# Two routing stages around an attention layer: PE's fillers, the top-six search and four shared products change places

## The reference

```python
x = x + 0.5 * ffn(layernorm(x))
x = x + attention(layernorm(x))
x = x + 0.5 * ffn(layernorm(x))

# ffn, on T = 2048 tokens of width 512, E = 64 experts, K = 6, CAP = 96
scores = sigmoid(x @ gate_w)                       # (T, 64)
scores_b = scores + bias
group_scores = sum of the two largest in each of 8 groups of 8
mask all but the 4 best groups
topk_ids = top_k(masked scores_b, 6); topk_w = scores at these ids
topk_w = topk_w / sum(topk_w) * 2.5
# each expert takes the first 96 tokens, in token order, that chose it
h = silu(buf @ w_gate) * (buf @ w_up)              # per expert, inner width 192
y = sum over the chosen experts of topk_w * (h @ w_down)
shared = (silu(x @ ws_gate) * (x @ ws_up)) @ ws_down
return y + shared
```

## Time and profile before

| | |
|---|---|
| median of 3 runs | 1400.79 us |
| profiled execution | 1399.98 us |
| its span, first to last instruction | 1397.8 us |
| PE busy | 1212.3 us (87%) |
| DVE busy | 620.0 us (44%) |
| ScalarE busy | 516.5 us (37%) |
| POOL busy | 507.5 us (36%) |
| mean granted clock of PE | 0.921 |
| read and written | 307.26 MB, mean 220 GB/s |

### The profile page before, as it was taken

How to read it: one execution, slowest core, us unless ns; L and a number is a source line. 1 busy time by engine, 2 the same in 40 slices (tenths; PEclk the granted TensorE clock), 3 DMA queues, 4 the chain that set the end, 5 groups by cost and what they waited for, 6 DMA issues and landing times.

```text
span 1397.8 us, 25616 instructions
## 1 busy us (share of the span) xinstructions
PE 1212.3 (87%) x10066; PEld 773.1 (55%) x10066; DVE 620.0 (44%) x1124; ACT 516.5 (37%) x1297; POOL 507.5 (36%) x413
## 2 busy tenths in 40 slices
PE   5999998888984668999999999889998998889880
PEld 4632776666762455565565565364435766657650
DVE  5775121221223676767867766533880221212220
ACT  1411211111110258888878878742211111111100
POOL 0022444544453643324324224000213544544544
PEclk9998999999997688899999999779986999999995
DMA  8995699999986934344444443232843999999957
GB/s 313 360 392 180 196 337 341 343 334 335 339 233 128 349 97 107 84 114 105 123 107 106 125 103 76 76 129 82 346 140 104 342 337 346 339 330 338 331 91 132
DMA packets 146199, 307.26 MB, mean 220 GB/s; under 512 B 17568, under 2 KB 50720, under 8 KB 146080
## 3 DMA queue, kind: packets, MB, share of 16 engines
q1 hardware_dynamic: 112960, 238.32, 50.5%
q0 software_dynamic: 23808, 57.69, 18.3%
q10 hardware_dynamic: 9312, 9.62, 2.0%
HBM read 222.47 MB, written 61.87 MB: 203 GB/s over the span
## 4 chain that ended last, share of the span: by engine, by line
PE 46%; DMA 27%; DVE 11%; issue 6%; ACT 4%; POOL 3%; SPq 1%; DVEq 0%; POOLq 0%; ACTq 0%
DMA ya_d<-osb,tok 13%; DMA out<-osb,tok 8%; PE ps L382 7%; PE ps L447 5%; PE ps L490 4%; DMA buf<-xn_d,tok 4%; PE ps L398 4%; PE ps L478 4%; PE ps L458 4%; PE ps L504 3%; PE ps L279 2%; PE ps L433 2%; DVE osb L976 2%; PE ps L365 2%; PE ps L271 1%
## 5 line engine op out<-in xcount | busy, mean ns | idle before, releaser
L382 PE MATMUL ps<-bufT,gu 128*64 128x96 f32 x6144 | 301.6, 261 | 0.0
L382 PEld LDWEIGHTS ps<-bufT,gu 128*64 128x64 f32 x6144 | 291.2, 176 | 9.2 <-issue 2.2
L976 DVE TENSOR_SCALAR osb<-ps,gt 96x512 f32<-96x512 f32 x128 | 94.1, 746 | 267.0 <-PE ps L398 75.2
L1045 DVE TENSOR_REDUCE Mx<-ps 128x1 f32<-128x512 f32 x256 | 170.4, 684 | 82.1 <-PE ps L458 81.4
L664 ACT COPY bufT<-ps 128x384 f32<-128x384 f32 x128 | 60.9, 478 | 346.1 <-PE ps L365 345.7
L704 ACT ACTIVATE ps<-ps,Mx 128x512 f32<-128x512 f32 x256 | 175.5, 688 | 35.7 <-DVE Mx L1045 34.9
L398 PE MATMUL ps<-wd,h 64*96 64x512 f32 x768 | 180.4, 602 | 3.2 <-DVE osb L976 3.2
L717 ACT ACTIVATE PT<-ps 128x512 f32<-128x512 f32 x256 | 159.0, 623 | 58.9 <-PE ps L478 57.7
L1161 POOL DMA_INDIRECT buf<-xn_d,tok x128 | 127.7, 998 | 93.9 <-issue 60.9
L458 PE MATMUL ps<-St 96*128 96x512 f32 x256 | 121.7, 490 | 19.5 <-ACT ps L704 18.8
L969 DVE TENSOR_TENSOR h<-sg,ps 128x288 f32<-128x288 f32 x64 | 29.1, 454 | 224.5 <-PE ps L382 224.5
(11 more groups left out here) (144 smaller groups left out, 1548.4 us busy)
## 6 DMA issues: line engine op xcount, KB each, us to landing
gu<-in_L_ffn_w_gate SPq DMA_DIRECT2D x64, 768.0 KB, 12.8
gu<-in_L_ffn_w_up SPq DMA_DIRECT2D x64, 768.0 KB, 15.7
wd<-in_L_ffn_w_down SPq DMA_DIRECT2D x64, 768.0 KB, 18.2
St<-HL SPq DMA_DIRECT2D x192, 128.0 KB, 2.3
wqk<-wp_d SPq DMA_DIRECT2D x32, 512.0 KB, 5.3
xn_d<-XN SPq DMA_DIRECT2D x24, 256.0 KB, 2.8
X<-in_L_attn_X SPq DMA_DIRECT2D x4, 1024.0 KB, 10.9
ya_d<-X SPq DMA_DIRECT2D x4, 1024.0 KB, 14.0
```

Of the source, the lines that this page charges most:

```text
L382: t = e.matmul(bk[64 * k:64 * k + 64, CAP * j:CAP * j + CAP], gu[:, 2 * k + m, c, j:F:3], f.bufT[(2 * q + k) % 4][:, c, :], start=(c == 0) ...
L976: e.tensor_scalar(f.osb[x % 4][:, :], bank(4 + x % 2)[0:CAP, :], f.gt[:, x % 8:x % 8 + 1], None, ALU.mult).then_inc(f_ev, 1)
L1045: e.tensor_reduce(Mx[:, qt, hl:hl + 1], bank((4, 5, 7)[n % 3]), AX, ALU.max, negate=True).then_inc(a_max, 1)
```

## The change

**PE, stage one.** Six products of X with itself into a bank that nobody reads (`pe_warm`) are issued when the first quarter of X has landed, and two more behind the first and the second group of four tiles. The gate part of shared group 0 stands behind the third group of tiles. The tiles are taken group by group right behind their root on DVE, ScalarE and PE; before, DVE was one group ahead. Three of the four weight splits move among them on ScalarE, the fourth behind the sigmoid, and its DVE part behind the key pass; SP stores that fourth part behind two expert loads.

**The top six.** The masked scores lie in rows of 66 columns, of which the last two are set to 3.0e38. The eight largest of a row are then these two and the six wanted. One `match_replace` puts 2.0e38 in the place of all eight, and "equal to 2.0e38" is the mask. The search for indices, the copy of the sixth index and four passes on DVE and three on POOL go; one pass on DVE and one on POOL come. The keys are smaller by the factor T and multiplied by T at the end.

**Shared expert.** Both stages use one order now: the keys' transposes stand before the last third of group 2, and all of group 0's down products behind it; the third multiply stands behind round 2 in both; the sums for the weights behind round 3. The list's transpose stands in the middle of group 2's down products. The four of group 3 go to the expert pairs: two behind the first gate and up product, two behind the first down product.

**The end of the attention.** The root of tiles 12 to 14 and these three tiles are issued on DVE before the last result, tile 15 has a root of its own, and PE does all of the rest of group 0 behind the logits.

The diff, cut to its core:

```diff
+        def pe_warm(e, n):
+            for _ in range(n):
+                e.matmul(bank(7), X[:, 0, 0:128], X[:, 0, :], start=True, stop=True)
+
         def pe(e):
+            e.wait_ge(s_x[0], 16)
+            pe_warm(e, 6)
             for g in range(4):
-                for i in range(4 * g - 4, 4 * g + 4 if g == 3 else 4 * g):
...
+                for i in range(4 * g, 4 * g + 4):
+                    pe_tile(e, f1, i)
+                    if i:
+                        pe_logits(e, f1, i - 1)
+                if g < 2:
+                    pe_warm(e, 2)
+                if g == 2:
+                    pe_shared_up(e, f1, 0, (0,))
...
             pe_attention(e)
-            pe_shared_up(e, f2, 0, (1, 2))
...
         def pe_route(e, f):
...
+            pe_shared_up(e, f, 0, (1, 2))
+            pe_shared_up(e, f, 1)
+            pe_shared_up(e, f, 2, (0, 1))
+            pe_keys(e, f)
+            pe_shared_up(e, f, 2, (2,))
+            pe_shared_down(e, f, 0)
+            pe_shared_down(e, f, 1)
+            pe_shared_up(e, f, 3)
+            pe_shared_down(e, f, 2, (0, 1))
+            pe_first(e, f)
+            pe_shared_down(e, f, 2, (2, 3))
...
         def pe_turned(e, f, x):
-            else:
-                e.wait_ge(f_shc, 16 * f.n + NT)
+            if x < 8:
+                e.wait_ge(f_shc, 16 * f.n + (12, 12, 14, 16)[x // 2])
...
         # pe_experts
+                if st in (1, 2):
+                    e.wait_ge(f_bTs, 64 * f.n + 2 * st + 2)
+                    pe_shared_down(e, f, 3, (2 * st - 2, 2 * st - 1))
...
         # act_route
+            e.preload_act_table(ACT.Sigmoid)
             e.wait_ge(f_lg, f.n + 1)
...
             if not f.n:
-                act_shared_silu(e, f, 0)
+                act_cast(e, 3)
...
         # dve_route
+            e.tensor_tensor(PM[:, :, 0:E].rearrange("p i (g j) -> p i g j", j=8), s8.rearrange("p (i g) j -> p i g j", g=NG),
+                            neg.rearrange("p (i g) -> p i g", g=NG).unsqueeze(3).to_broadcast([128, NT, NG, 8]), ALU.add)
+            e.memset(PM[:, :, E:E + 2], BIG).then_inc(f_step, 1)
...
             for i in range(NT):
+                t = e.match_replace(PM[:, i, :], f.V8[:, i, :], PM[:, i, :], MARK)
...
+            e.scalar_tensor_tensor(out=P1, in0=PM[:, :, 0:E], scalar=MARK, in1=bE(cst[:, C_TK:C_TK + 16]),
+                                   op0=ALU.is_equal, op1=ALU.add).then_inc(f_step, 1)
...
-                if r == 5:
+                if r == 3:
...
-                if r == 2 and not f.n:
+                if r == 2:
                     dve_shared_mul(e, f, 2)
...
         # dve_attention
+                    if u == NU and j == 12:
+                        dve_root(e, f2, 1)
+                        for i in range(12, 15):
+                            dve_tile(e, f2, i)
...
         # sp
+            for c in range(3):
+                store_part(e, c)
...
+            e.wait_ge(s_wd, 16 * 6)
+            for q in (1, 2):
                 load(e, f1, q)
+            store_part(e, 3)
             e.wait_ge(s_y, 64)
             load(e, f1, 4)
+            e.wait_ge(s_wd, 16 * 8)
+            load(e, f1, 3)
```

More of the change, by code:

```diff
@@ L755, in act @@
                 act_root(e, f1, g)
-                for i in range(4 * g - 4, 4 * g + 4 if g == 3 else 4 * g):
-                    if i >= 0:
-                        act_tile(e, f1, i)
-                        if i in (9, 11, 13, 15):
-                            c = i // 2 - 4
-                            e.wait_ge(s_wf[c], 16)
-                            e.copy(wh[c][:, :], wf[c][:, :].bitcast(F32)).then_inc(w_hi, 1)
+                for i in range(4 * g, 4 * g + 4):
+                    act_tile(e, f1, i)
+                    if i in (5, 8, 10):
+                        act_cast(e, (5, 8, 10).index(i))
             act_route(e, f1)
@@ L768, in act @@
             act_root(e, f2, 1)
-            act_shared_silu(e, f2, 0)
-            for i in range(12, NT):
+            for i in range(12, 15):
                 act_tile(e, f2, i)
+            act_root(e, f2, 2)
+            act_tile(e, f2, 15)
             act_route(e, f2)
@@ L841, in part @@
                 return flat(ap)[:, o:o + m * j].rearrange("p (m j) -> p m j", j=j)
-            if f.n:
-                dve_shared_mul(e, f, 0)
-            else:
+            if not f.n:
                 e.wait_ge(s_c, 32)
@@ L930, in dve_route @@
+            if not f.n:
+                dve_rest(e, 3)
             e.wait_ge(f_kT, f.n + 1)
@@ L1143, in dve @@
             dve_attention(e)
-            dve_root(e, f2, 1)
-            for i in range(12, NT):
-                dve_tile(e, f2, i)
+            dve_root(e, f2, 2)
+            dve_tile(e, f2, 15)
             dve_route(e, f2)
@@ L1375, in sp @@
             load(e, f1, 0)
-            store_parts(e)
+            for c in range(3):
+                store_part(e, c)
             for g in range(4):
```

181 lines of the change are left out of this document (68 added, 113 removed).

## The result

In paired runs the changed kernel took 1384.93 us (median of 13, 1374.52 to 1399.56) beside 1405.18 us for the kernel before (1393.35 to 1413.62): ratio 0.9875, 95% interval 0.9844 to 0.9907. The ratio is formed from the fast executions alone, so it is not the quotient of the two medians (0.9856). Forecast was 1386, range 1373 to 1398. The first profile of it, however, is of an execution of 1398.34 us (span 1396.5), only 1.3 us of span under the profile before (1397.8). So two profiles have to be compared stretch by stretch; each pair of end times would tell another story.

What follows compares the result with a forecast made beforehand. The expert stages' scatter-adds, with DMA saturated, were taken as the bound, so their start, set by the routing before, counts. The terms 11.0 + 4.9 - 2 = 14 us off 1399.98 gave 1386 us, range 1373 to 1398.

Steps and rivals of the forecast that it cites:

- L: End of the last router logits: forecast 46 us in stage one, against 53.7 before.
- the DVE stall: Key search, behind round 2: VectorE waits 4.3 us for the first four shared products before the third shared multiply.
- F: The list's transpose after the key search: forecast 110.8 us in stage one, a gain of 14.2.
- P0: End of the experts' first down product: forecast 141.3 us in stage one, a gain of 16.3.
- P1: End of the experts' second down product: forecast 154.2 us in stage one, a gain of 11.4.
- A: Start of the attention layer's first product; 11 us was taken as stage one's gain that reaches the end.
- R to K: Stage two, start of the attention layer's last result products to end of the key transposes: forecast 49.0 us.
- rival 1: The gap before the list's transpose does not lower TensorE's clock: 6 us a stage, 1374 us; chance 0.12.
- rival 2: Stage one's router tiles do not hold 2.4 GHz: 1412 us if all slow, chance 0.08; about 1397 if half, 0.12.
- The second scatter-add: Expert stage: it waits for the last shared result, some 6 us behind P0, which costs nothing.
- rival 3: Expert weights become the wait, or DMA engines run dry: 6 to 8 us given back, 1393 us; chance 0.15.
- The sum of 14: Whole kernel: 11.0 from stage one plus 4.9 from stage two minus 2 for clock falls, off 1399.98 us.

Runs made afterwards that it cites:

- e5: Changed kernel with the last four shared products put back ahead of the experts in both stages; ratio 0.9931 to the kernel before.
- e3: Changed kernel with three filler products in TensorE's idle time before the list's transpose, both stages; ratio 0.9892 to the kernel before.
- e4: Changed kernel with the third shared multiply moved from behind round 2 to behind round 4, both stages; ratio 0.9932 to the kernel before.
- e7: Changed kernel with the third multiply behind round 4 and the sixth expert pair's load held until two gathered blocks are transposed; ratio 0.9818 to the kernel before.
- e1: The changed kernel run again without edits, for a second profile; ratio 0.9913 to the kernel before.
- e2: Changed kernel without the ten warm products of stage one; ratio 0.9979 to the kernel before.
- e12: The kernel before the change, run again without edits for a second profile; that execution took 1412.3 us.
- e10: Changed kernel with third multiply behind round 4, sixth pair's load held, router weights earlier, and attention rows ahead of shared weights; ratio 0.9882 to the kernel before.
- e11: Changed kernel with only the sixth expert pair's load held until the first two gathered blocks are transposed; ratio 0.9918 to the kernel before.
- e6: Changed kernel with 5.5 us of VectorE passes that nobody reads added ahead of the key pass, both stages; ratio 0.9983 to the kernel before.

## Why the prediction was right

**Stage one, right in mechanism.** In the first profile: tiles at full clock from the first logits on, L 46 for 44.3, match_replace 3.2 for 3.15, the DVE stall, PE idle 3.6 for 3.37, F 110.8 for 108.6, P0 141.3 for 139.6, P1 154.2 for 152.7. The stall behind round 2 was 2.67, not 4.3: the last weight part's pass (2.60 beside GpSimd, not 1.76) stood between the key pass and the rounds, and delayed the rounds before they could wait. F-K hardly notices (38.3 for 38.9), because the stall ends where PE's first four products end. In stage two, which has no such pass, it was 4.02. In the second profile L was 49.0 and P1 157.7, and the gain at A 7.9 instead of 12.3; the 11 that I took lies between.

**Stage two, too much.** R to K is 52.4 us in both profiles, not 49.0. Two terms: L comes 1.0 later than I had it, and the matmuls behind the last gap run slow, which costs the 2.4 us that L to K takes more than in stage one (28.3 for 25.9). I had this as a subtraction of 2. P1-R gained 1.0 to 2.4, where 4.9 - 2 = 2.9 stood.

**The move of four products, right in sign.** e5 prices it by the profiles, 5 us a stage; the times leave it open. I had priced the pairs, not the move.

**No fall at F (rival 1), wrong in price.** I gave 6 us a stage if the gap passed. e3, e4 and e7 took the gap away, and against e1 P0-F came out 2.0 less (e3), 1.3 more (e4) and 1.1 less (e7) in stage one and within 0.2 in stage two, since the gather is next. I had written that the gather was hidden by the copy of a shared result; that held only as long as the products were slow.

**Slower tiles (rival 2), present.** Not the whole stretch, but from a wait of about 2 us to the next fillers, in five of nine profiles, 3 to 5 us each. The Trainium skill (TensorE: Matmul & The Clock Gate, Part 4: PE-mode transpose) has transposes not counting as busy in the same way. Here tiles that are one third transposes, with fillers between the groups, kept 2.4 GHz for 28 us once they had it (first profile). Without help they needed 28 us to get it in e2 and 31 in the first profile of before, which agrees with the page, but 7 us in e12, which does not. So the traces do not settle the rule: tiles can bring the clock up by themselves, and what makes it 7 us or 28 is open.

**The second scatter-add** waits for the last shared result, as I had it (four profiles name its store, `yb_d<-XN`, as what ended the wait), but comes 14.0 us behind P0 (153.70 for 139.7), not 6. I wrote that this costs nothing, since the third cannot start before P1 anyway. That is not shown, and there are signs against it. In those four (e2, e4, e10, e11) it was issued 0.5 to 0.7 us ahead of P1; there PE waits 1.6 us for DVE to empty a bank in stage one, and P1 to A is 287.6 to 288.8. In the other seven with the moved products it was issued 0.6 to 1.4 us behind P1; there these waits are 4.8 to 8.4 us and P1 to A is 288.8 to 292.5. No run changed this alone, and before and e5, where it comes 3.2 us ahead of P1, have 290.5 to 293.0, so the cause stays open.

**The experts' weights (rival 3)** were never waited for, and P1 to A is the same before and after within 2 us.

The sum of 14 was right partly by luck: the profiles give 12.3 and 2.4 (first), 7.9 and 1.0 (second), and the medians moved by 20 and 13 us in two comparisons. What the single parts are worth does not add up to the whole either: leaving out the warm products (e2) and putting back as much DVE work as the top six lost (e6) cost 0.7% each, and the whole change brought 0.9 to 1.25%.

## What to carry to other kernels

Cut two profiles at the same events and compare the stretches, before reading any end time: one stretch here has two lengths, 12 us apart, in both kernels. Before you price the removal of a gap, ask what the slow work behind it covers; that will be the next wait. Short independent filler that starts when the first data lands was worth as much here as 5.5 us of VectorE work in each stage (0.7% each), but a wait of 2 us behind it undid half of that; so look at what the work behind the filler waits for.

## What the runs showed of the hardware

- Behind the warm products the tiles kept the full clock in all six profiles in which PE then waited 0.2 to 1.1 us (first profile: 1.10, then 1.08 us for eight router matmuls), and ran at the low level in all five in which it waited 1.9 to 2.4 us (e1: 2.00, then 1.73 and 1.81). In e12 tiles without fillers lost it behind 1.57 and 1.55 us.
- The same kind of tiles, without warm products, came to the full clock 7 us behind the first of them in e12, 28 us in e2 and 31 us in the first profile of before.
- Shared products kept the low level for 24 us after one gap of 3.37 us, although PE had work all the time (e5, twelve groups of 2.07 us); the next dense expert products brought the high one back.
- From the same waits near the attention layer's end the clock came back after 12 us or not within 37, with the same instructions between them.
- PE could take up the first indirect gather of 96 rows 7.2 us after its issue with a 2.3 MB load issued 2.4 us ahead of it (e4), 4.9 us with that load 5 us ahead (e3), and 3.7 us with none (e7).
